# Normalising in parts and reordering ScalarE's copies in a deformable convolution, attention and expert kernel

## The reference

```
x = x + deform_conv(group_norm(x))        # 9 taps: offsets by a 3x3 convolution, two cells gathered and
                                          # weighted for each tap (bilinear), then a 128x128 product per tap
t = tokens(x)                             # 3136 tokens of 128 channels for each image
a = layer_norm(t)
q, k, v = a Wq^T, a Wk^T, a Wv^T
t = t + softmax(causal(q k^T / sqrt(128))) v
f = layer_norm(t)
p = softmax over the tokens of (f gate_w + gate_b)       # 64 experts
topv, topi = the 8 best tokens of each expert
pooled = sum of their f rows, weighted with topv
out = expert(pooled)                      # gelu(pooled W1 + b1) W2 + b2
t = t + scatter_add(out * topv at topi)
```

## Time and profile before

| | |
|---|---|
| median of three runs | 2978.67 us (2977.55 to 2979.96) |
| the profiled execution's own time | 2981.11 us |
| its span | 2979.3 us |
| busy: TensorE matmul / weight load | 90% / 71% |
| busy: VectorE, ACT, GpSimd | 64%, 60%, 59% |
| mean granted clock of TensorE, 1 is 2.4 GHz | 0.967 |
| ACT: scaling of one tap (L547), mean | 0.391 us, x1800 |
| ACT: copy of a sample piece (L552), mean | 0.487 us, x600 |
| three such copies back to back | 1.24 us |
| ACT: copy of a probability chunk (L566), mean | 0.547 us, x728 |
| ACT: exponential of a row (L639), mean | 1.676 us, x200 |
| VectorE: second cell of a tap (L800), mean | 0.346 us, x1800 |

### The profile page before, as it was taken

One profiled execution on the slowest core, in us unless ns is written; L12 is line 12 of the kernel. 1 busy time (PEld: TensorE's weight loads), 2 busy tenths in 40 slices (PEclk: granted clock), 3 DMA queues, 4 the chain that ended last, 5 costly groups with the idle time before them and its releaser, 6 DMA issues. The chain is left out here.

```text
span 2979.3 us, 52944 instructions
## 1 busy us (share of the span) xinstructions
PE 2691.2 (90%) x18970; PEld 2122.1 (71%) x18970; DVE 1898.5 (64%) x7132; ACT 1773.7 (60%) x4046; POOL 1769.2 (59%) x1837
## 2 busy tenths in 40 slices
PE   5788999999999999999999999999999997999575
PEld 3566877778767877778767877778777786777452
DVE  3466666867487666867587666766587657664324
ACT  2555666666666666666666666666666666664320
POOL 5777775775477655775477655775477656720000
PEclk8899999999999999999999999999999998999787
DMA  7454334633254324633265324633254323412397
GB/s 186 119 147 137 112 105 125 160 115 92 79 160 138 105 82 125 160 116 90 85 159 138 100 86 129 160 114 90 88 153 145 100 84 111 118 50 80 106 398 298
DMA packets 221235, 383.22 MB, mean 129 GB/s; under 512 B 44570, under 2 KB 131546, under 8 KB 220460
## 3 DMA queue, kind: packets, MB, share of 16 engines
q0 software_dynamic: 89856, 255.58, 29.6%
q1 hardware_dynamic: 126955, 109.28, 12.3%
q10 hardware_dynamic: 4160, 14.98, 1.3%
HBM read 317.04 MB, written 62.65 MB: 127 GB/s over the span
## 5 line engine op out<-in xcount | busy, mean ns | idle before, releaser
L521 POOL DMA_INDIRECT shared<-pair_table,idx x1800 | 1744.8, 969 | 873.9 <-issue 528.3
L1107 PEld LDWEIGHTS bank_o<-vals,prob_t 128*128 128x128 f32 x5200 | 635.5, 192 | 179.6 <-ACT prob_t L566 114.8
L1107 PE MATMUL bank_o<-vals,prob_t 128*128 128x128 f32 x5200 | 670.2, 277 | 72.9 <-ACT prob_t L566 72.0
L810 DVE CUSTOM_DVE_ANT_0 prob<-bank_r,mask 128x512 f32<-128x512 f32 (+3 forms) x728 | 451.9, 629 | 348.0 <-PE bank_r L1085 346.5
L566 ACT ACTIVATE prob_t<-bank_r 128x512 f32<-128x512 f32 (+3 forms) x728 | 382.8, 547 | 487.9 <-PE bank_r L1094 487.0
L1085 PE MATMUL bank_r<-keys,qt 128*128 128x512 f32 (+3 forms) x1456 | 632.1, 550 | 0.0
L547 ACT ACTIVATE shared<-shared,wa 128x128 f32<-128x128 f32 x1800 | 561.5, 391 | 36.4 <-DMA shared<-pair_table,idx 36.4
L800 DVE SCALAR_TENSOR_TENSOR shared<-shared,wb 128x128 f32<-128x128 f32 x1800 | 514.6, 346 | 105.5 <-ACT shared L547 104.0
L1074 PEld LDWEIGHTS bank_r<-convw_t,smp_t 128*128 128x128 f32 x3600 | 452.3, 198 | 89.6 <-ACT smp_t L552 53.1
L1074 PE MATMUL bank_r<-convw_t,smp_t 128*128 128x128 f32 x3600 | 487.5, 283 | 31.6 <-ACT smp_t L552 31.6
L1094 PE MATMUL bank_r<-ident,prob 128*128 128x128 f32 x2600 | 385.7, 275 | 1.0 <-ACT prob L639 1.0
(11 more groups left out here) (154 smaller groups left out, 2194.8 us busy)
## 6 DMA issues: line engine op xcount, KB each, us to landing
shared<-in_dram SPq DMA_DIRECT2D x32, 1024.0 KB, 17.8
shared<-pair_table,idx POOLq DMA_INDIRECT x1800
pair_table<-rows_out SPq DMA_DIRECT2D x112, 256.0 KB, 3.1
t<-in_dram SPq DMA_DIRECT2D x48, 256.0 KB, 4.0
t_dram<-t SPq DMA_DIRECT2D x48, 256.0 KB
shared<-in_dram SPq DMA_DIRECT2D x7, 1568.0 KB
stage<-t_dram POOLq DMA_DIRECT2D x8, 832.0 KB, 7.4
pm_dram<-logit SPq DMA_DIRECT2D x8, 800.0 KB, 10.2
```

Source lines behind the costliest of these rows:

```text
L521: pool.indirect_dma_start(g[t % RING][:, n, :], None, pair_table[b % 2], bass.IndirectOffsetOnAxis(ap=idx[:, b % 2, i * TAPS + n:i * TAPS ...
L810: dve.tensor_tensor_reduce(prob_at(t, k0, w), ring_bank(("score", t, c))[:, 0:w], m, 1.0, NEG, ALU.add, ALU.max, cmax[t % 2][:, c:c + 1]). ...
L1107: last = pe.matmul(attn_ps, prob_t[q % 3][:, n * P:(n + 1) * P], vals[:, slot(tb, at), :], start=(at == 0), stop=(at == ti))
```

## The change

It has four edits.

1. `normalise` takes a part of the image, 14 of its 56 rows (784 columns), and PARTS = 4 calls take the place of one. In step 4 of an image one part is issued after each round from the second on (after that round's probability copy and scaling piece); what is left follows the uses at "L", where the whole normalisation stood. Ahead of the loop the four parts stand one after the other. `turn_rows` and the offset convolution wait for the part that holds their last row.
2. Where the score tile has one chunk (steps 6 to 9 of an image), ACT copies the three sample pieces ahead of the exponential.
3. `early` begins at three chunks instead of four: in steps 15 to 18 the scaling pieces come after the second and third probability copies (and after the uses at "M") instead of ahead of them. VectorE's order stays.
4. In step 12 the first turned expert probabilities move from place E to M, the second from M to L, behind the keys.

```diff
+PARTS = 4
...
-    (12, "E", "pm", -1, 0), (12, "F", "turn", 1, 3), (12, "M", "pm", -1, 1), (12, "L", "keys", 0, 2),
+    (12, "F", "turn", 1, 3), (12, "M", "pm", -1, 0), (12, "L", "keys", 0, 2), (12, "L", "pm", -1, 1),
...
-            def normalise(k):
+            def normalise(k, part):
+
                 after(affine_done, k + 1)
-                inner = xpad[:].rearrange("p (y x) -> p y x", x=XW)[:, 1:1 + H, 1:1 + W]
-                given = first_image.rearrange("p (y x) -> p y x", x=W) if k == 0 else inner
+                y0, y1 = part * H // PARTS, (part + 1) * H // PARTS
+                inner = xpad[:].rearrange("p (y x) -> p y x", x=XW)[:, 1 + y0:1 + y1, 1:1 + W]
+                given = first_image.rearrange("p (y x) -> p y x", x=W)[:, y0:y1, :] if k == 0 else inner
                 act.activation(inner, given, ACT.Identity, bias=nb[:, 0:1], scale=rs[:, 0:1]).then_inc(normalised, 1)
...
-            normalise(0)
+            for part in range(PARTS):
+                normalise(0, part)
...
+                samples_first = step < ALL and chunks_in(step - LAG_S) == 1
+                if samples_first:
+                    for p in range(PIECES):
+                        keep_samples(step, p)
                 if 0 <= v < ALL:
...
-                if step < ALL:
+                if step < ALL and not samples_first:
                     for p in range(PIECES):
                         keep_samples(step, p)
...
-                early = chunks_in(v) >= 4
+                parts = list(range(PARTS)) if s == NORMALISE and b + 1 < B else []
+                early = chunks_in(v) >= 3
...
                     if early and pieces:
                         scale_first(step + 1, pieces.pop(0))
+                    if c >= 2 and parts:
+                        normalise(b + 1, parts.pop(0))
                 for p in pieces:
                     scale_first(step + 1, p)
                 for use in misc_at(step, "L"):
                     keep_misc(use)
-                if s == NORMALISE and b + 1 < B:
-                    normalise(b + 1)
+                for part in parts:
+                    normalise(b + 1, part)
...
-                after(normalised, k + 1)
+                after(normalised, PARTS * k + (8 * n + 7) * PARTS // H + 1)
...
-                    after(normalised, b + 1)
+                    after(normalised, PARTS * b + min(8 * n + 8, H - 1) * PARTS // H + 1)
```

## The result

The changed kernel takes 2963.22 us (median of six runs, 2961.51 to 2965.43), the kernel before 2978.66 beside it: a ratio of 0.9946, 95% interval 0.9936 to 0.9957. That is 15.4 us faster, where 31 were forecast, and 1.2 us beyond the slow end of the range.

The account below looks back on a forecast made before the run. TensorE, busy 90% of the span, sets the pace, waiting mostly on ACT's copies. 21.9 + 3.1 + 1.5 + 3.4 + 1.4 = 31.3 us off 2981.11 gives 2949.8, as runs' median 2947.5; range 2932 to 2962.

Parts of the forecast that it names:

- Part 1: Step 4: the 2.4 us wait goes in six images, with 1.5 us of clock in five; 21.9 us won.
- It just fits: Step 4: ACT has room for four parts of 1.0 us; the fourth ends at 1441.0, keys due at 1441.12.
- Part 2: Step 6: TensorE's wait moves from 2.4 to 1.8 us, 0.45 us in each of seven images; 3.1 us won.
- the better end that the range allowed for: Step 6: 2 us an image where the clock fell behind the old wait.
- Part 3: Steps 15 to 18: wins 0.5, 0.6 and 0.4, loses 1.3 in step 17; 0.2 us an image, 1.5 for eight.
- Rival C: Steps 15 to 18: more, shorter waits lower the clock twice an image; 24 us given back, 2971; chance 0.05.
- my own bound of 6: Whole kernel: changes under 0.2% (6 us) can't be told from none.
- E: Steps 15 to 18: last sum late in all four steps; 43 us lost, 13 us slower, 2992; chance 0.06.
- First image: Step 15 of the first image: last samples turned at 243.9 instead of 247.8; 3.4 us more than counted.
- the term of 1.4 us: Kernel start: transposes begin after one normalised part, so the gathers start 1.4 us sooner (bounds 0.5 and 2.1).
- Part 4: Step 12: the 1.21 us wait goes, a 0.6 wait for keys comes; nothing, -0.3 to +0.4 us an image.

Follow-up runs that it names:

- part 1 alone: Only the normalisation in four parts, put into the kernel before: 2961.30 us, ratio 0.9943.
- part 3 alone: Only the scaling between copies in steps with three pieces, put into the kernel before: 2980.95 us, ratio 1.0010.
- the wait taken out: The changed kernel with VectorE copying the turned offsets of step 12 ahead of its layer norm: 2947.81 us, ratio 0.9892.
- both mends: The changed kernel with step 12's offset copy ahead of the layer norm and the first piece scaled ahead of the query copy in steps 17, 21: 2934.23 us.
- Part 2 alone: Only the samples ahead of the exponential in steps with one chunk of scores, put into the kernel before: 2968.73 us, ratio 0.9971.
- the query copy late: The changed kernel without part 4, ACT scaling the first sample piece ahead of the query copy in steps 17 and 21: 2929.67 us, ratio 0.9833.
- the four parts alone: Four kernels, each the kernel before with one of parts 1 to 4: 2961.30, 2968.73, 2980.95 and 2984.78 us.

## Why the prediction was wrong

The direction and the mechanism of each of the first three parts came out; the time did not, since 15.4 us were lost in a step (part 4) that I had priced at nothing.

**Part 1, right.** The parts take 1.04 us (taken: 1.0), the keys copy was not late, the wait of 2.4 us went without a new one, and the 12 products took 1.50 us: 23.2 us for 21.9. "It just fits" was as tight as it sounds: 0.18 us were left. What I missed is that part 1 alone does not keep all of it: without part 2 the clock falls one step later.

**Part 2, right in kind, too small.** The moved wait is 1.79 us (1.8). I had 0.45 us an image; it is 0.6, and the clock that used to fall there in the third image held (2.1 us); the last image won 1.6. 7.6 us for 3.1, the better end that the range allowed for.

**Part 3, right in the waits.** -0.4 to -0.6, -0.7, +1.4 and -0.4 to -0.6 us for -0.5, -0.6, +1.3 and -0.4. In step 17 TensorE waits 0.91 us for the first sum:

```profile
1591.96 0.55 PE L1077 MATMUL bank_r<-ident,shared 128*128 128x128 f32 x3 [0.91 <-DVE shared L811]
```

Rival C, that the new short waits lower the clock, was true here at 1.7 us a fall (1.5 forecast), in three images instead of twice in each. I had set against it that the matmuls around waits of up to 1.7 us ran at full rate. That was a count of waits that had gone well, and part 3 alone shows how near they were: five falls in eight images. It was due a larger chance than 0.05, and the same question in step 12, where I did not ask it. C was also filed wrongly: its 2971 is 7 us below the kernel before, over my own bound of 6, so it belonged to "faster". (And E's terms, four times 1.3 for eight images, make 41.6, not 43, so 2990.5 for 2992.) The Trainium skill (TensorE: Matmul & The Clock Gate, "A second HAM failure mode") describes frequent short idles between groups of matmuls that make the clock swing. The traces agree in kind: the clock falls around waits of 0.91, 0.35 and 0.30 us in step 17, and of 1.55 and 0.69 in step 12. They also show the same waits with the clock up.

**First image.** The last sample turn of step 15 ended at 247.8 us and now ends at 242.9 (243.9 forecast). The start shows nothing in this pair of traces: GpSimd's first gather starts at 36.21 us for 36.33, and it is released by the store of the rows:

```profile
36.21 1.14 POOL L522 DMA_INDIRECT shared<-pair_table,idx  x1 [26.63 <-DMA pair_table<-rows_out]
```

But one pair misleads here. In the traces on chips of this kind the first gather starts at 34.98 to 36.21 us in the six kernels with four parts (mean 35.5) and at 36.33 to 37.37 in the four without (mean 36.8), behind the stores in some and the indices in others of either sort. So at the gathers the term of 1.4 us is there. What it is worth later can't be read: the first addition stands at 70.4 us before, at 72.5 and 72.4 in parts 2 and 3 alone, which leave the start as it was, and at 74.9 in part 1 alone.

**Part 4, the step that failed.** "Nothing, between -0.3 and +0.4 us an image." The waits came out inside those bounds: 0.2 us where the clock holds. Two things failed. I took the end of VectorE's chain as what decides and saw that it does not move, but did not ask what the moved turn itself waits for: the shared bank, which VectorE empties only behind the layer norm, 1.55 us. And I priced a wait at its length. Where the clock holds, the two new waits in place of the old one cost 0.2 us; where it comes down, the 10 us behind them cost 2.5 us more. Of the 15.4 us 11.6 lie in images 2 to 7: 1.4 for the waits (six times 0.23), the rest with the clock. The 3.9 of the last image come with part 4 but not with the wait of 1.55 us, which it doesn't have; what brings the clock down there stays open. With the wait taken out the changed kernel measures 2947.81 us, without part 4 2949.11, which is the forecast of 2947.5, though by terms that partly cancel: part 2 gave more, part 3 and the first image less.

## What to carry to other kernels

A wait of an engine whose clock follows its work has two prices, its length and the clock behind it. When a change shortens one wait and makes others, list the waits of about 1 us and more, and the rows of shorter ones, that are left or new behind it, and bound each by a fall (here 1.5 to 3.2 us), not by zero. And when an instruction is moved ahead in a shared buffer's order, ask who empties the buffer before it and what stands ahead of that copy in its engine's program: here one reordered copy on VectorE was worth 15 us.

## What the runs showed of the hardware

- The same instructions with the same waits leave the clock up in one image and bring it down in the next: step 12 at 10.60 and 13.19 us in the changed kernel, 9.87 and 12.99 with both mends. Part 2 alone leaves a wait of 2.39 us untouched and has fewer falls behind it. What decides between them no row here shows. In step 17 with the query copy late it stays up in all eight images of both kernels that have it.
- Falls move. With the wait taken out of step 5, the clock fell in step 6 of six images instead of one. Single gains don't add: the four parts alone give -16.4, -8.9, +3.3 and +6.5, whose sum of -15.5 meets the measured -15.4 only because the first three are worth 7.2 us more together and the fourth costs 7.6 more beside them. That the moving falls are the whole reason is argued, not shown.
- Chips differ in kind: the same kernel takes 2978 us on some and 3960 to 4095 on others, with matmuls waiting for "issue", and there leaving out part 4, which brings the kernel to 1% below the one before on the first kind, gives nothing.
